# Score stacks in two strips of heads, with a changed order of groups, of shift rows and of the tail's weighing

## The reference

```
x = x + xattn(layernorm(x), ctx)
  Q, K, V = proj(q, Wq, bq), proj(k, Wk, bk), proj(v, Wv, bv)      # 16 heads of 8
  scores  = Q K^T / sqrt(8) + m[h] * softplus(1000 + |i - j|)       # a slope for each head
  x       = softmax(scores) V;  return x Wo^T + bo
x = x + ffn(layernorm(x))
  shared  = silu(x Sg) * (x Su) Sd
  probs   = softmax(x Wr); the top 2 of 16 give the weights c
  routed  = sum over e of c[e] * (silu(x Wg[e]) * (x Wu[e])) Wd[e]
```

## Time and profile before

| | before |
|---|---|
| median of 3 runs | 241.05 us (240.48 to 241.5) |
| profiled execution | 241.2 us, span 239.4 us |
| mean granted clock of PE | 0.986 of full speed |
| PE busy | 217.2 us, 91% of the span |
| DVE, ACT, POOL busy | 174.7, 119.0, 75.4 us |
| shift pass matmuls L379 | 256, 23.7 us, one alone 219 ns |
| second pass matmuls L437 | 256, 25.6 us, one alone 224 ns |
| one exponential L747 (ACT) | 592 ns |
| one seed L994 (DVE) | 686 ns |
| one tanh, gate, hidden | 384, 413, 412 ns |
| one chunk weighed by POOL L1315 | 729 ns |
| one low part L958 (DVE) | 473 ns |
| shift rows (SP), first issue | at 21.43 us, read by PE at 23.57 |

### The profile page before, as it was taken

The page is one execution under the profiler, slowest core; times in us unless marked ns, Lnnn a source line. Parts: engine busy times, 40 slices in busy tenths (PEclk is TensorE's granted clock), DMA queues, the critical chain, the costliest instruction groups (busy, mean ns, idle before and its releaser), DMA issues.

```text
span 239.4 us, 6083 instructions
## 1 busy us (share of the span) xinstructions
PE 217.2 (91%) x1942; PEld 177.2 (74%) x1942; DVE 174.7 (73%) x610; ACT 119.0 (50%) x283; POOL 75.4 (31%) x180
## 2 busy tenths in 40 slices
PE   2989387888999999999999999999999989989995
PEld 2667244676789788887888787887897779868985
DVE  4689504699579966996799678967896689654791
ACT  8475423647443654366336633574446434753420
POOL 2510002401193109410770068014900390029000
PEclk9999959999999999999999999999999999999999
DMA  5553566032704170144314340335032700160000
GB/s 155 164 93 103 133 162 233 4 100 51 175 1 104 52 181 17 57 95 124 77 43 103 92 107 4 96 96 149 3 101 58 191 0 4 50 154 1 1 25 22
DMA packets 13079, 20.24 MB, mean 85 GB/s; under 512 B 2800, under 2 KB 9440, under 8 KB 12544
## 3 DMA queue, kind: packets, MB, share of 16 engines
q1 hardware_dynamic: 12624, 18.77, 30.3%
q10 hardware_dynamic: 432, 1.19, 1.5%
HBM read 16.03 MB, written 3.78 MB: 83 GB/s over the span
## 4 chain that ended last, share of the span: by engine, by line
PE 46%; issue 29%; POOL 10%; DVE 5%; DMA 4%; ACT 3%; SPq 0%; DVEq 0%; POOLq 0%; ACTq 0%
PE ps_m L549 9%; PE ps_up L523 8%; POOL hid L1315 6%; PE ps_pv L456 5%; PE ps_st L437 4%; PE ps_up L528 4%; DVE nmax L975 3%; PE ps_pv L463 3%; PE ps_s L379 2%; DMA stacks_sb<-qk_dram 2%; PE ps_st L491 2%; PE ps_st L397 1%; DMA ident<-in_c_ident 1%; PE ps_m L478 1%; ACT probs L747 1%
## 5 line engine op out<-in xcount | busy, mean ns | idle before, releaser
L799 ACT ACTIVATE th<-ps_up 128x256 f32<-128x256 f32 x72 | 27.7, 384 | 39.0 <-PE ps_up L528 38.5
L747 ACT ACTIVATE probs<-ps_st 128x512 f32<-128x512 f32 x64 | 36.8, 592 | 16.9 <-PE ps_st L437 16.7
L549 PE MATMUL ps_m<-wd_sb,hid 128*128 128x128 f32 x288 | 44.8, 283 | 0.0
L975 DVE TENSOR_REDUCE nmax<-ps_s 128x4 f32<-128x512 f32 x64 | 42.0, 680 | 0.8 <-issue 0.4
L1079 DVE SCALAR_TENSOR_TENSOR tg<-th,ps_up 128x256 f32<-128x256 f32 x72 | 29.7, 413 | 13.3 <-ACT th L799 12.5
L1315 POOL TENSOR_TENSOR hid<-hid,crep 128x256 f32<-128x256 f32 x56 | 39.1, 729 | 0.2 <-issue 0.2
L549 PEld LDWEIGHTS ps_m<-wd_sb,hid 128*128 128x128 f32 x288 | 37.6, 191 | 1.0
L1085 DVE TENSOR_TENSOR hid<-tg,ps_up 128x256 f32<-128x256 f32 x72 | 29.7, 412 | 1.0
L523 PE MATMUL ps_up<-x_hi,wg_hi 128*128 128x256 f32 x72 | 26.6, 369 | 0.4 <-ACT x_hi L780 0.2
L437 PE MATMUL ps_st<-stacks_sb 98*128 98x128 f16 x256 | 25.6, 224 | 0.4 <-DMA stacks_sb<-nmT 0.3
L1279 POOL TENSOR_TENSOR ve<-mv,eps_sb 128x1 f32<-128x1 f32 x16 | 3.0, 191 | 71.5 <-DVE mv L1026 71.5
(11 more groups left out here) (147 smaller groups left out, 446.6 us busy)
## 6 DMA issues: line engine op xcount, KB each, us to landing
crep<-cw_dram SPq DMA_DIRECT2D x28, 256.0 KB, 4.6
stacks_sb<-qk_dram SPq DMA_DIRECT2D x32, 128.0 KB, 3.3
qk_dram<-qk_parts SPq DMA_DIRECT2D x16, 128.0 KB, 1.8
out_y<-x_all SPq DMA_DIRECT2D x8, 128.0 KB, 4.6
wg_sb<-in_wgT ACTq DMA_DIRECT2D x1, 576.0 KB, 3.5
wu_sb<-in_wuT ACTq DMA_DIRECT2D x1, 576.0 KB, 3.3
wd_sb<-in_wd SPq DMA_DIRECT2D x1, 576.0 KB, 4.9
x_all<-in_x SPq DMA_DIRECT2D x2, 256.0 KB, 3.3
```

Of the source, the lines that this page charges most:

```text
L549: last = mm(ps_dn[:, b * P:(b + 1) * P], hid[:, buf, c, b * P:(b + 1) * P], wd_sb[:, c, :], start=(c == 0 and b == 0), stop=(c == SHARED), ...
L747: fn(probs[:, b, g * HG * P:(g + 1) * HG * P], scores_bank(a, g)[:], ACT.Exp).then_inc(exp_sb, 1)
L799: fn(th[:, c % 2, :], ps_up[c % 2][:, 0, :], ACT.Tanh, scale=0.5).then_inc(tanh_sb, 1)
L975: v.tensor_reduce(nmax[:, b, HG * g:HG * g + HG], ps_s[g % 2][:].rearrange("p (h j) -> p h j", h=HG), AX_X, ALU.max, negate=True).then_inc ...
```

## The change

The stacks get two strips. Strip 0 starts at row 0 and holds heads 0 to 7, strip 1 starts at row 64 and holds heads 8 to 15; each has 32 rows of parts and 2 rows of shift or ones. The zero rows and the fills of whole stacks are gone. The shift pass uses 32 rows of a strip, the second pass 34. A stack is filled by 8 DMAs of half the size (before 4), the shift rows of an item by 2 DMAs (before 1). Groups are taken in the order of heads 0, 2, 1, 3 (in fours), so that the strips alternate. Calls take a tuple of groups; two calls of a step have two groups in it, whose matmuls are issued in turn, and all others have one.

```diff
 SROWS = 4 * DH
-ZROWS = 96
-AROWS = ZROWS + 2
+AROWS = SROWS + 2
+HS = H // 2
+ORDER = (0, 2, 1, 3)
...
-        stacks_sb = sb("stacks_sb", [AROWS, 2, 2, H, T], F16)
+        stacks_sb = sb("stacks_sb", [STRIP + AROWS, 2, 2, HS, T], F16)
...
             def shift_rows(a, b, buf):
                 sp.wait_ge(nm_sb, 2 * a + b + 1)
-                sp.dma_start(qs[buf][ZROWS:AROWS, :, b * P:(b + 1) * P], nmT[:, b, :]).then_inc(s_nm[b], 16)
+                for s in range(2):
+                    sp.dma_start(qs[buf][STRIP * s + SROWS:STRIP * s + AROWS, :, b * P:(b + 1) * P],
+                                 nmT[H * s:H * (s + 1), b, :]).then_inc(s_nm[b], 16)
...
             def step(f, a, p, q, abuf):
-                if at_start(a): shift_rows(a, 0, abuf)
+                if at_start(a):
+                    shift_rows(a, 0, abuf)
+                    shift_rows(a, 1, abuf)
                 if p is not None: write_parts(p, 1 - abuf)
                 if not at_start(a): shift_rows(a, 0, abuf)
                 if p is not None: stack_k(p, 1 - abuf)
-                shift_rows(a, 1, abuf)
+                if not at_start(a): shift_rows(a, 1, abuf)
...
+                for k in range(HG):
+                    for i in groups:
+                        row, h = STRIP * (i % 2), HG * (i // 2) + k
+                        last = mm(ps_s[i % 2][:, k * P:(k + 1) * P], qs[buf][row:row + SROWS, h, b * P:(b + 1) * P],
+                                  ks[buf][row:row + SROWS, h, b * P:(b + 1) * P], start=(i > 0), stop=True,
+                                  skip_group_check=True)
```

`scores_T` has the same loop with `AROWS` rows. In a step's PE order the calls become `scores(a, 0, (0, 1))` and `scores_T(a, 1, (1, 2))`, and the down product of chunk 8 goes behind the first group of the second item:

```diff
+                scores_T(a, 1, (0,), abuf)
                 if not at_start(f): down(f - 1, (8,), abuf)
-                scores_T(a, 1, 0, abuf)
                 weigh_values(a, 0, f)
-                scores_T(a, 1, 1, abuf)
-                scores_T(a, 1, 2, abuf)
+                scores_T(a, 1, (1, 2), abuf)
                 values_T(a, 0)
```

The second seed of a step waits for one exponential more and stands behind `hidden(f, 5)` on DVE:

```diff
             def seed(a, g):
-                dve.wait_ge(exp_sb, 2 * NHG * a + NHG + g - 1)
-                v.tensor_copy(ps_st[(g + 1) % 2][:], bias_T[:, g, :]).then_inc(seed1_sb, 1)
+                dve.wait_ge(exp_sb, 2 * NHG * a + NHG - 1 + 2 * g)
+                v.tensor_copy(ps_st[1][:], bias_T[:, g, :]).then_inc(seed1_sb, 1)
```

```diff
             keep_clock(6, ps_st[1][:, 0:P])
             down(f - 1, (0, 1), 1 - last, f)
-            keep_clock(6, ps_st[1][:, 0:P])
+            down(f - 1, (2, 3), 1 - last, by_dve=2)
             expert_in_T(f)
-            keep_clock(3, ps_st[1][:, 0:P])
+            keep_clock(5, ps_st[1][:, 0:P])
             up(f, 0)
-            down(f - 1, (2,), 1 - last)
             router(f)
             up(f, 1)
-            down(f - 1, (3,), 1 - last)
             up(f, 2)
...
             hidden(f - 1, 8, 1 - last)
+            weigh_late(2)
+            weigh_late(3)
             x2_low(f)
...
-            for pair in range(1, PAIRS):
+            for pair in range(2, PAIRS):
                 weigh_experts(NG - 2, pair, (NG - 2) % 2)
```

More of the change, by code:

```diff
@@ L366, in scores @@
                         pe.wait_ge(own, 6)
[L367 to L371, removed]
-                    pe.wait_ge(v_sb, a + 1)
[L373 to L382, removed]
+                if b == 0 and 1 in groups:
+                    pe.wait_ge(v_sb, a + 1)
+                if b > 0 or groups[-1] > 1:
+                    pe.wait_ge(max_sb, n + groups[-1] - 1)
+                if 0 in groups:
+                    mm(ps_s[0][:], dist16[:], slope_hi[:, 0:HG, :], start=True, stop=False, skip_group_check=True)
+                for k in range(HG):
[4 more added lines that the diff above has]
+                                  skip_group_check=True)
+                        if k == HG - 1:
+                            last.then_inc(s_mm, 1)
             def shift_T(a, b):
@@ L433, in scores_T @@
                         pe.wait_ge(act_pads, 2)
-                first = False if seeded else bias(bank, g)[0]
-                for h in range(HG * g, HG * g + HG):
-                    o = (h - HG * g) * P
-                    last = mm(bank[:, o:o + P], ks[buf][:, h, b * P:(b + 1) * P], qs[buf][:, h, b * P:(b + 1) * P],
-                              start=first, stop=True, skip_group_check=True)
-                    first = False
-                last.then_inc(st_mm, 1)
+                    elif isinstance(a, int) and a == 1:
+                        pe.wait_ge(act_pads, 4)
+                first = {i: False if seeded[i] else bias(scores_bank(a, i), ORDER[i])[0] for i in groups}
+                for k in range(HG):
+                    for i in groups:
+                        row, h = STRIP * (i % 2), HG * (i // 2) + k
+                        last = mm(scores_bank(a, i)[:, k * P:(k + 1) * P], ks[buf][row:row + AROWS, h, b * P:(b + 1) * P],
+                                  qs[buf][row:row + AROWS, h, b * P:(b + 1) * P], start=first[i], stop=True,
+                                  skip_group_check=True)
+                        first[i] = False
+                        if k == HG - 1:
+                            last.then_inc(st_mm, 1)
             def weigh_values(a, b, f=None):
@@ L865, in _ @@
             act.wait_ge(zero_sb, 2)
-            fill(stacks_sb[:, 0, 1], zero)
-            act.wait_ge(act_pads, 1)
-            act.wait_ge(dve_pads, 1)
-            fill(ks[0][ZROWS:AROWS], ones16)
+            for s in range(2):
+                fill(ks[0][STRIP * s + SROWS:STRIP * s + AROWS], ones16)
             act.wait_ge(s_ctx, 16)
```

195 lines of the change are left out of this document (101 added, 94 removed).

## The result

The changed kernel takes 253.96 us (median of 4 runs, 250.18 to 255.32) where the kernel before takes 240.95 on the same chip: a ratio of 1.044, 95% interval [1.033, 1.056]. The ratio takes only the two faster of the four runs (250.18 and 253.17 us), since the other two, at 254.75 and 255.32 us, lie over 1.5% above the fastest; the medians of all runs give 1.054. It is slower, as forecast.

What follows compares the result with a forecast made beforehand. From step 1 to 7 time was taken as what TensorE has to issue. Strips +13.3, first step -2.5 and tail -0.5 sum to +10.3: 251.5 us profiled, 251.4 median; own range 245 to 257, 244 to 257 with B's low end.

Steps and rivals of the forecast that it cites:

- The switch: TensorE, between strip blocks and whole-array work: 0.09 us going in, 0.14 coming out, 14 and 12 times, 2.94 us a step.
- The pairs: Two pairs of score groups a step, issued in turn on two strips, run at once: 0.45 us a step saved.
- What the waits absorb: Of the switches' 2.94 us a step, 0.6 falls where TensorE waits now (bounds 0.2 and 1.0).
- Order and transfers at nothing: Steady steps: new group order and second seed taken as 0; more DMA issues fit where SyncE idles over half the time.
- the cover that I named: Second seed's chain, about 1.5 us, hides behind TensorE's down(8) and value weighing, about 1.6; uncovered, 0.1 to 0.5 a step.
- The start: First score matmul waits for the last stack, issued about 1.3 us later but half as long: +0.5 us (bounds 0 and 1.3).
- First step: Shift rows go out at once, shortening TensorE's idle stretch; a later x load takes back 1.7: -2.5 us (bounds -4.2 and 0).
- the very sign that I had named: If TensorE's clock is at half after 28 us, the first step's term is wrong.
- Tail: Last half step: down(2) and down(3) replace six filler transposes and leave the ups: -0.5 us (bounds -0.8 and 0).
- A, the free switch: Switch costs nothing for these strips, or costs only where weights are float32: 234.9 us, faster; chance 0.08.
- B, swallowed: Switch price is right but the trace's waits swallow it, 26 x 0.09 with 1.0 absorbed: 242.3 us; chance 0.14.
- C, the weights within a strip: Next weights cannot load beside the running matmul in a strip: 1.6 us a step, 11 more in all, 262.5; chance 0.07.

Runs made afterwards that it cites:

- changed kernel without switches: The changed kernel with both score passes reading all rows of the stacks for every group, zero rows between the strips: 243.41 us, ratio 1.011.
- SyncE's order alone: The kernel before with only SyncE's order in the first step changed, both items' shift rows issued ahead of group 1's writes: 237.50 us, ratio 0.983.
- the 32-row kernel: The kernel before with only the shift pass's matmuls reading rows 0 to 31 of the stacks, not 0 to 95: 247.62 us.

## Why the prediction was right, point by point

**The switch.** The mechanism and both prices hold: 0.10 going in (0.54 for 0.44), and 0.15 coming out where I had 0.14 (0.55 for 0.40 up to the second L529; into L557 0.10 to its first start and 0.05 more within it). For 14 ways in and 12 ways out this gives, as an estimate from these starts, 2.8 to 3.0 us a step (the way out into L505 costs 0.10, and the one into L469 is hidden by its wait); I had 2.94. The Trainium skill, "TensorEngine Tiling (Array Packing)", section "Tiling Modes", has the engine drain at such a change; these traces agree, with those 0.10 and 0.15 us, and show the same cost with strips of 32 and of 64 rows.

**The pairs.** 0.22 us for the first is there, for the second it is hidden by ScalarE. The reason was half wrong: two groups overlap because they lie on different strips, and need not be issued in turn for it.

**What the waits absorb.** With one or both savings taken off, 2.4 to 2.8 us of issue are added a step, and a step grew by 1.8. So 0.6 to 1.0 went into waits, where I had 0.6; with the first pass alone on strips it was 0.9 where I had 0.3. TensorE's idle time fell by 0.2 a step only (2.4 to 1.5 over five steps), but that count misses the short waits. The new wait for the seed is in the 1.8 too, so that the net came as close as 1.8 for 1.9 is in part luck. In step 1 the difference was 0.9, with TensorE's idle time the same 2.7 us in both kernels; why that step loses less I did not take apart. The strips sum to 11.8 us in place of 13.3.

**Order and transfers at nothing.** This holds only under the cover that I named. Without the switches they cost 0.9 us a step. The bounds of the seed's wait, 0.1 to 0.5, were stated; that the second shift transfer would keep the second pass waiting in a steady step (0.3 us) I had not seen: I had looked at SyncE's share of idle time, not at who waits for the last of the issues.

**The start.** +0.5 was wrong in sign: -0.6. (The sum has no term for it; the -2.5 of the first step is worked out in times from the beginning, with the late stack in them.) The stacks' transfers are half as long (2.2 us to landing for 64 KB, 3.3 for 128, by the pages of the two profiles). Part may be the fills after all: with two zero fills back, the first score matmul starts at 16.94 instead of 16.38 and 16.44. Kernels with whole fills start at 16.7 to 17.4, so this is likely and not shown. That the fills end long before the first score matmul was misread: the largest runs from 12.84 to 16.31 us on VectorE (L1206), and the matmul starts at 17.03.

**First step.** Restart at 28.54 (28.7 forecast), copy at 25.80 (26.5), x issued at 33.24 (32.7), statistics of x at 36.58 (residual forecast for 36.9): the chain of x came as worked out, and start and first step together gave -2.9 where the sum has -2.5. That this is so close is partly luck. The second weighing of values starts at 34.99, 3.3 us sooner than before and not 4.2, and only 0.5 us is given back behind it and not 1.7. The claim of a full clock failed, by the very sign that I had named. TensorE had idled for 0.84 and 1.05 us shortly before 29.3, and the clock fell to half, for 3.4 us in one run and 10.2 in another. The step of it that failed: "after an idle stretch of some 1 us, hence at full clock". Yet the changed kernel without switches idled for 0.84 and 0.94 us at the same two places and kept its full clock, so idle stretches of this length do not settle it; what does stays open. The half clock is why the median is 254 and not 250, as far as the two traces show it, and with 3.8 us it is larger than any other miss. The step also gives up what the order earns: SyncE's order alone gets this step to 20.76 us, the changed kernel to 23.16, and x is issued at 33.24 instead of 29.56, with four shift transfers and eight of the stacks ahead of it.

**Tail.** 0 instead of -0.5. Only the up's wait for its buffer was under-priced; the bound was 0.

**The sum.** 251.5 was forecast for the profiled execution and 250.18 came: strips -1.5, start and first step -0.4, tail +0.5. The median came 2.6 above the forecast, since the clock added what no term had. The two misses have opposite signs: without the first, the median would have come 3.8 us above the forecast. So part of its closeness is luck.

**Rivals.** A, the free switch: refuted by one slice (32 rows, 3.6 us in five steps at full clock). B, swallowed: the absorption comes near its 1.0, but its price of 0.09 for the way out is too low. C, the weights within a strip: a block of four takes 0.32 with its exit and eight on one strip 0.54, so the pace inside is still that of before. The Trainium skill, "TensorE: Matmul & The Clock Gate", "The mechanism", lets a load overlap only when its row group differs; the blocks do not show it: the eight L379 of the 32-row kernel's pair, all on the same rows and each with its own weights, start 0.056 us apart, and one load takes 0.09. The gain of up to 2x that the Trainium skill, "TensorEngine Tiling (Array Packing)", section "Theoretical Speedup", has for small dimensions of at most 64 shows in the first pass's pair, 0.22 for 0.45 us without the way out, and in no single block.

## What to carry to other kernels

Where small matmuls on part of the array alternate with whole-array ones, count the changes of division, not the rows: here about 0.25 us from start to start for each block of four, which four matmuls of 0.056 cannot earn back. Two groups side by side on different strips did run in half the time, interleaved or not; it is the short blocks that lose. A cost may hide another: after taking one away, look at the waits again before booking its whole price. When a distance in the timeline is to be a price, look first whether its far end waits for another engine. And of a change with several parts, run each alone: one line of SyncE's order was worth -4 us inside a change worth +13.

## What the runs showed that I had not expected

TensorE's granted clock went to half (1.2 of 2.4 GHz) after idle stretches of 0.84 and 1.05 us with 0.9 us of work between them, and how long it stayed there differed between runs of the same kernel (3.4 us, and 10.2 us with another 3.4 later). After stretches of 0.84 and 0.94 us in the kernel without switches it did not fall. Two groups on different strips overlap even when they are issued one after the other: 0.34 us up to the next instruction, the switch on the way out included, against 0.32 interleaved and 0.45 on the whole array with no switch at all.
